# Decomposed queries and keys laid out by dimension in DRAM, narrower key loads, and the maxima stored by SyncE

## The reference

```python
q = x @ Wq
latent_kv = (x @ Wk + x @ Wv) @ W_down_kv
k_rec, v_rec = latent_kv @ W_up_k, latent_kv @ W_up_v     # 16 heads of 8 dimensions
scores = clip(einsum('bhqd,bhkd->bhqk', qh, kh) * scale)
scores = clip(scores * exp(-0.01 * 0.01 * abs(i - j)))     # decay by distance
out = softmax(scores) @ vh
```

## Time and profile before

| | us |
|---|---|
| median of 3 timed runs | 937.31 (935.65 to 938.31) |
| profiled execution, its own time | 933.09 |
| profiled execution, span of the core | 931.6 |
| TensorE busy in the span | 765.9 (82%) |
| DVE, ACT, POOL busy | 603.1, 481.9, 268.0 |
| first attention within the span | from 0 to about 450 |

### The profile page before, as it was taken

One profiled execution on the slowest core, in us unless ns is written; L12 is line 12 of the kernel. 1 busy time (PEld: TensorE's weight loads), 2 busy tenths in 40 slices (PEclk: granted clock), 3 DMA queues, 4 the chain that ended last, 5 costly groups with the idle time before them and its releaser, 6 DMA issues. The chain is left out here.

```text
span 931.6 us, 26320 instructions
## 1 busy us (share of the span) xinstructions
PE 765.9 (82%) x10923; PEld 472.2 (51%) x10923; DVE 603.1 (65%) x1402; ACT 481.9 (52%) x966; POOL 268.0 (29%) x590
## 2 busy tenths in 40 slices
PE   5469999999999999998747939999995894127990
PEld 3226555555555555554525925666653463025770
DVE  3666888888888888885362233777767445762444
ACT  4717888888878888877522543434332322001222
POOL 2547434333333343334106613000000000005531
PEclk9657999999999999998867969999999796557995
DMA  5433321111111111000292119000000003001104
GB/s 155 151 114 122 120 72 55 55 55 55 56 55 55 54 55 54 6 4 4 68 293 76 43 56 303 1 1 1 1 2 1 0 1 128 11 0 42 42 23 147
DMA packets 39319, 59.12 MB, mean 63 GB/s; under 512 B 10100, under 2 KB 21053, under 8 KB 39200
## 3 DMA queue, kind: packets, MB, share of 16 engines
q1 hardware_dynamic: 34352, 51.07, 17.0%
q0 software_dynamic: 2304, 4.74, 2.0%
q10 hardware_dynamic: 2544, 1.62, 0.6%
HBM read 42.09 MB, written 15.07 MB: 61 GB/s over the span
## 5 line engine op out<-in xcount | busy, mean ns | idle before, releaser
L857 DVE CUSTOM_DVE_ANT_0 junk<-row,rest 128x1024 bf16<-128x1024 f32 x256 | 312.7, 1225 | 71.2 <-PE row L388 53.6
L641 ACT ACTIVATE prob<-score 128x512 f32<-128x512 f32 x512 | 274.4, 598 | 89.9 <-PE score L388 89.4
L388 PE MATMUL score<-stack 75*32 75x128 bf16 (+3 forms) x3840 | 180.6, 300 | 6.1 <-DMA stack<-neg_rows 4.8
L502 PE MATMUL out_ps<-prob,v_aug 128*32 128x256 f32 x2048 | 158.4, 387 | 1.6 <-POOL prob L768 1.6
L388 PE MATMUL row<-stack 72*32 72x512 bf16 x1928 | 150.2, 387 | 0.7
L768 POOL TENSOR_SCALAR_AFFINE_SELECT prob<-prob 128x128 f32<-128x128 f32 x256 | 79.0, 309 | 199.8 <-ACT prob L641 195.2
L388 PEld LDWEIGHTS score<-stack 75*32 75x32 bf16 x3840 | 93.5, 98 | 70.2 <-ACT prob L641 15.3
L502 PEld LDWEIGHTS out_ps<-prob,v_aug 128*32 128x32 f32 x2048 | 63.4, 112 | 52.9 <-issue 2.4
L1773 POOL MEMSET ones<- 128x128 bf16 x2 | 0.4, 205 | 233.9 <-POOLq L1214 214.6
L388 PEld LDWEIGHTS row<-stack 72*32 72x32 bf16 x1928 | 48.6, 98 | 29.5 <-DVE top L857 5.2
L2006 PE MATMUL outs<-vm_w,mixed 128*64 128x256 f32 x512 | 61.7, 381 | 1.8 <-issue 1.8
(11 more groups left out here) (305 smaller groups left out, 1053.6 us busy)
## 6 DMA issues: line engine op xcount, KB each, us to landing
stack<-parts_dram SPq DMA_DIRECT2D x64, 288.0 KB
parts_dram<-prob SPq DMA_DIRECT2D x12, 256.0 KB, 7.4
parts_dram<-spare SPq DMA_DIRECT2D x12, 256.0 KB
results<-x_tok SPq DMA_DIRECT2D x12, 256.0 KB, 3.7
up_w<-in_L_ffn_w_dram SPq DMA_DIRECT2D x1, 2048.0 KB, 9.6
rows<-x_tok SPq DMA_DIRECT2D x8, 256.0 KB, 3.5
y<-results SPq DMA_DIRECT2D x8, 256.0 KB, 4.1
up_w<-in_L_ffn_wg_dram SPq DMA_DIRECT2D x1, 2048.0 KB, 10.4
```

Of the source, the lines that this page charges most:

```text
L388: last = pe.matmul(out[c:c + 32, :], keys[:, c:c + 32], queries, start=True, stop=True)
L502: last = pe.matmul(out_ps[32 * c:32 * c + 32, h // 2 * (S // 4):(h // 2 + 1) * (S // 4)], v_aug[g % 3][:, t, h, :], moving[:, :, c, :], st ...
L641: act.activation(prob[:, t, w * HALF:(w + 1) * HALF], score[n % NS][:, :], ACT.Exp).then_inc(exped, 1)
L857: dve.tensor_tensor_reduce(junk[:, slot % 2, :], row[slot % 2][:, :], rest[:, S - P - t * P:2 * S - P - t * P], 1.0, LOWEST, ALU.mult, ALU ...
```

## The change

`parts_dram` changes from (side, half, group, 24 rows, head in group, position) to (side, half, 24 rows, group, head in group, position). The projection weights are reordered so that a batch's 128 partitions go by dimension and then head, not by group, dimension and head in group. A store of one piece then writes 8 rows of 16 heads. Rows of one piece lie 64 KB apart (8 KB before). The query load keeps its form; the key load becomes three loads of 24 rows without a broadcast, and a stack's semaphore counts four DMAs (LOADS = 1 + NPART) instead of two. The table `rest` is loaded by ACT behind the ramps, at the front. `store_neg` moves from ACT to SP: heads 0, 1 and 2 between the early loads, the others between the four sides of a pair's loads in the loop. The second side of a pair (n = 1) waits for 3 units where it waited for 6. The general path addresses the new layout.

```diff
 def load_side(sp, dram, stack, pair, half, side, loaded):
-    h, group = 2 * (pair % 2), pair // 2
-    rows = dram["parts"][side, half, group, :, h:h + 2, :]
+    h, group, of = 2 * (pair % 2), pair // 2, NPART * HD
+    rows = dram["parts"][side, half, :, group, h:h + 2, :]
     if side == 0:
-        rows = rows.unsqueeze(1).to_broadcast([NPART * HD, NPART, 2, S])
+        sp.dma_start(stack[0:KR, half, 0, h:h + 2, :], rows.unsqueeze(1).to_broadcast([of, NPART, 2, S])).then_inc(loaded, 16)
     else:
-        rows = rows.unsqueeze(0).to_broadcast([NPART, NPART * HD, 2, S])
-    sp.dma_start(stack[0:KR, half, side, h:h + 2, :], rows).then_inc(loaded, 16)
-LOADS = 2
+        for a in range(NPART):
+            sp.dma_start(stack[a * of:(a + 1) * of, half, 1, h:h + 2, :], rows).then_inc(loaded, 16)
+LOADS = 1 + NPART
...
         def send_part(sp, b, half, side, k, done):
-            rows = dram["parts"][side, half, b * (NG // B):(b + 1) * (NG // B), :, :, :]
+            rows = dram["parts"][side, half, :, b * (NG // B):(b + 1) * (NG // B), :, :]
             if side == 0:
-                rows = rows[:, k * HD:(k + 1) * HD, :, :].rearrange("g r h t -> g (r h) t")
+                rows = rows[k * HD:(k + 1) * HD, :, :, :].rearrange("r g h t -> r (g h) t")
             else:
-                rows = rows.rearrange("g (r k) h t -> (g r) k h t", k=NPART)[:, k, :, :]
+                rows = rows.rearrange("(r k) g h t -> r k (g h) t", k=NPART)[:, k, :, :]
             sp.dma_start(rows, parts[b][half][:, side, k, :]).then_inc(done, 16)
...
             store_parts(sp, 0, 0, 0, 0, kept[0][0])
-            sp.dma_start(rest[:, :], io["c_rest"]).then_inc(rest_in, 16)
             for k in range(1, NPART):
...
+            def store_neg(m):
+                tile, h = of_head(m)
+                sp.wait_ge(row_done, slot_at["neg", m] + 1)
+                for half in range(2):
+                    sp.dma_start(tile[KR:KR + NPART, half, 0, h, :].rearrange("k (t c) -> k t c", c=P),
+                                 neg_rows[:, m % 2, :]).then_inc(neg_in[m % 2], 16)
...
+            store_neg(0)
             sp.wait_ge(rows_set, 2)
             for n in range(4):
                 fill_side(2, n, 0)
+            store_neg(1)
             for n in range(4):
                 fill_side(3, n, 0)
+            store_neg(2)
...
-                if pair + 3 < PAIRS:
-                    for n in range(4):
-                        fill_side(pair + 3, n, 2 * UNITS * pair + 6 * n)
+                for n in range(4):
+                    if n in (2, 3):
+                        m = 2 * pair + n - 1
+                        if n == 3 and pair + 3 < PAIRS:
+                            fill_side(pair + 3, 2, 2 * UNITS * pair + 12)
+                        if m < NH:
+                            store_neg(m)
+                    if n != 2 and pair + 3 < PAIRS:
+                        fill_side(pair + 3, n, 2 * UNITS * pair + 3 * n + (9 if n == 3 else 0))
...
             for n in range(2):
                 act.dma_start(ramp[n], io["c_ramp"][:, n, :]).then_inc(ramp_in, 16)
+            act.dma_start(rest[:, :], io["c_rest"]).then_inc(rest_in, 16)
...
-            store_neg(0)
             for step in range(LAST):
                 m, t = step // SB, step % SB
-                if t == 4 and m + 1 < NH:
-                    store_neg(m + 1)
...
             def by_head(w):
-                return w.rearrange("d (g h r) -> d g r h", h=GH, r=HD)
+                return w.rearrange("d (n r) -> d r n", r=HD)
             def by_dimension(w):
-                return w.rearrange("d (g r h) -> d g r h", h=GH, r=HD)
+                return w.rearrange("d (r n) -> d r n", r=HD)
```

More of the change, by code:

```diff
@@ L990, in _ @@
                         sp.dma_start(queries[a * NPART * HD:(a + 1) * NPART * HD, :],
-                                     parts[0, 0, g, a * HD:(a + 1) * HD, h, :].unsqueeze(0).to_broadcast([NPART, HD, S])).then_inc(loaded, 16)
+                                     parts[0, 0, a * HD:(a + 1) * HD, g, h, :].unsqueeze(0).to_broadcast([NPART, HD, S])).then_inc(loaded, 16)
                         for k in range(NPART):
                             at = (a * NPART + k) * HD
-                            sp.dma_start(keys[at:at + HD, :], parts[1, 0, g, k:NPART * HD:NPART, h, :]).then_inc(loaded, 16)
+                            sp.dma_start(keys[at:at + HD, :], parts[1, 0, k:NPART * HD:NPART, g, h, :]).then_inc(loaded, 16)
         @block.tensor
@@ L2241, in two_layers @@
             mem[f"returned{i}"] = sem(f"returned{i}")
-        dram = {"parts": nc.dram_tensor("parts_dram", (2, 2, NG, NPART * HD, GH, S), BF16, kind="Internal").ap()}
+        dram = {"parts": nc.dram_tensor("parts_dram", (2, 2, NPART * HD, NG, GH, S), BF16, kind="Internal").ap()}
         for i in range(2):
```

## The result

| | before | after |
|---|---|---|
| median of 19 timed runs of each, us | 941.27 (935.65 to 947.34) | 932.74 |
| ratio, 95% interval | | 0.9903 (0.9882 to 0.9923) |
| span of the profiled execution, us | 931.6 | 931.2 |

The change makes the kernel 9.1 us faster (7.2 to 11.1, one minus the ratio, times 941.27); forecast were 10.0.

A forecast was written before the change was run, and what follows sets the result against it. The prediction took the loop to run at TensorE's pace behind a late first score; 9.0 us from the start plus 1.0 from the loop took 937.31 to 927.3 us, range 921 to 933.

The forecast's parts named there:

- One sign of being wrong: Main loop and start: the prediction called itself wrong if TensorE stands before a head waiting for its maxima.
- Step 1: Stores of pieces to DRAM: outer dimension 8 gives 1.37 us each, bounds 0.97 and 2.7 us.
- Step 2: Key loads: one of 288 KB becomes three of 96 KB, 0.36 us each; an issue 0.79 us, perhaps 0.43.
- Step 3: Decay table at the front on ACT's queue: cost 0, at most 3.6 us lost.
- Step 4: The start, summed: key issues from 28.8, first row matmul at 32.9, first score 54.0 instead of 63.01, gain 9.0 us.
- Step 5: Main loop: stores of maxima by SP free ACT and gain 1.0 us, bounds 0 and 2.6.
- Step 7: TensorE's clock: its lag of 16.7 us behind the first score moves with the start, no further gain or loss.
- Rival A: TensorE's clock doesn't follow the start and comes back at 79.7 as before: 4.5 us lost, 931.8 us; chance 0.11.
- Rival B: Start and loop gain more: issues at 0.43 us, clock 4 us sooner, loop at its bound: 922.7 us; chance 0.10.
- C: Key loads don't spread: each 96 KB load stays at 76 GB/s, 1.3 us; 930.3 us; chance 0.05.
- D: Rows 64 KB apart in DRAM are served worse, start's stores keep 2.7 us each: 941.9 us; chance 0.05.
- E: Gain eaten behind the attention, where the clock can dip otherwise: 935 to 938 us, no change; chance 0.05.

The follow-up runs named there:

- e2: Kernel before with only each 288 KB key load split into three of 96 KB, old layout: -6.5 us (-9.6 to -3.4).
- e1: Kernel before with only the decay table loaded by ACT behind the ramps: -2.1 us (-4.8 to +0.6).
- g3: f2 with the decay table again loaded by SP behind the first store: 920.25 us, -11.7 (-14.8 to -8.4) against the kernel before.
- f1: Changed kernel with all stores of maxima issued by ACT again: -11.0 us (-14.0 to -8.1) against the kernel before.
- f2: Changed kernel with SP storing head 0's maxima between the half 1 loads of pairs 0 and 1: 918.30 us, ratio 0.9868.
- f0: Changed kernel unedited, run once more: 924.74 us against 930.13 for the kernel before, ratio 0.9933 (0.9896 to 0.997).
- before again: Kernel before unedited, run once more for a second trace: -1.1 us (-3.5 to +1.2).
- e4: Kernel before with only the stores of maxima moved from ACT to SP: +17.7 us (+13.5 to +21.8).
- e3: Kernel before with only the new DRAM layout, keys still in one broadcast load: -4.4 us (-7.1 to -1.6).
- f3: Changed kernel with room for nine groups in DRAM, rows 72 KB apart instead of 64 KB: 924.40 us, -7.2 (-10.5 to -3.7) against before.
- g2: f2 in the DRAM layout of the kernel before: 924.89 us, ratio 0.9912 (0.9881 to 0.9944) against the kernel before.

## Why the prediction was right, step by step

The forecast was 10.0 us faster, measured 9.1 and 6.2. The direction and the place (the start, and how many engines carry a transfer) were right. That the size comes so close is in part luck: the gain of the start was forecast too large, that of the loop didn't come, and a clock that came back sooner than forecast made up for some of it. The forecast time of 927.3 us was worked out from 937.31, the median of three runs; nineteen runs gave 941.27, and so 932.74 lies only just inside the range of 921 to 933. One sign of being wrong that the prediction named did come: TensorE stands 4.6 us before head 0 for its maxima, where the sum had 1 us.

Step 1, stores of 1.37 us: 1.30 measured (262,144 B at 202 GB/s). Step 2, narrow loads: issues of 0.35 us, under the lower bound (0.43) I gave; their transfers slower than 270 GB/s (168 at a share of 0.76 in e2). Step 3, table at no cost at the front: right, and worth little, as e1 and g3 show.

Step 4, the key issue at 28.8: wrong by 2.4 us. I took five stores to follow each other at 1.37 us. They nearly do so in half 1, where the queue is full (1.3 us each from 38 to 44), but not in half 0: the last lands 5.6 to 6.5 us after its issue in all versions of the new layout, where my sum had 3.5. The old layout with the table away has 5.2 to 5.7, so for half 0 the new layout brought nothing. A reason at hand is that it widens the query stores (share 0.25 alone before, 0.53 now) and narrows the key stores (in their stretch of the kernel before, 26.0 to 27.5, the share is 0.90 at 279 GB/s); no run tests this by itself. The bounds I set (0.97 to 2.7 us per store) covered the delay, but I used them as if the cost was in the engine's time per store. Three issues at 0.35 us made good for it: pair 1's issues end at 34.6, forecast 34.4. The six stores of half 1 then cost 1.5 us more than forecast: SP goes on at 46.43 and not at 44.7, since their packets pass between 36.7 and 46.0, which is 9.3 us and not 8.2, and begin 0.7 us later than I had them, beside the last loads.

Step 4, the maxima: the largest miss, 3.0 us. I had the second store land 1.7 us after its issue and the first score 2.2 us after it; the score came 5.2 us after it (53.02 to 58.23), behind eight loads in one queue. The 256-byte packets of the maxima pass between 55.42 and 56.48, so 1.75 us of the 5.2 lie behind their last byte. Without the wait (f1 and f2) the first score comes 3.9 and 3.2 us sooner than f0's on the table's scale, and the times are 5.3 and 6.4 us lower. More than the 3 to 4 us can't be put down to this wait: the attention ends only 1.5 and 0.6 us sooner than in f0's trace, 3.5 and 2.6 sooner than in the mean of the two. My text named these loads as new work in front of the maxima, counted their issues (6.4 us, measured 5.7) and forgot their bytes. Together 9.0 us were forecast and 4.8 measured in the first pair of traces; from the last key store on, over both traces of each kernel, it is 6.4.

Step 5, the loop's 1.0 us: it was next to nothing. Four heads take 47.44 to 47.47 us with and without ACT's issues (means over six groups in before, after, f0, f1, from the seventh turn of the maxima on), so that eight groups differ by some 0.2 us. The 0.13 us in one score group were not a cost repeated in each group of heads, and an ACT that is nearly full (94% with its issues) is not the bound.

Step 7, the clock: I let its lag of 16.7 us move with the first score. In the other thirteen traces it came back 8.6 to 16.7 us after the first score, but 34 to 41 us after it fell, save for before again (44.4) and e4 (51.2). The first trace of before had 47.8. So after the change the clock was back 7.4 us sooner and not 4.8, which explains most of the 6.7 us by which the attention ends sooner: (4.8 + 7.4) / 2 = 6.1, as half a us counts for each at the lower level. The clock also falls once near the end of the loop, for 6.8 us before and 3.4 us after the change, and in the second trace of either kernel not at all. Rival A, the clock back at 79.7, fell.

Rival B's cheap issues came, its other gains didn't. C fell: the loads spread (share 0.76 in e2, 0.67 here beside the maxima). D fell: stores take 1.3 us. Its argument from the single key load holds only roughly (76/3 is 25.3 GB/s per engine, 270/12 is 22.5), and rows further apart are not wholly free for the loads, as the last section shows. E came about in the one pair of profiles, by chance and not because of the shift: the wait of 3.7 us shown above is missing in the second trace of the same kernel.

What stays open: why the last five stores of half 0 need 11 to 12 us from the second one's issue to the key load (after the change the engines move 66 GB/s at a share of 0.47 from 20.7 to 22.0 and reach 199 GB/s only at 26, at about the same share); why the clock came back so soon in e3; and where the difference between 9.1 and 6.2 comes from, whose intervals overlap.

## What to carry to other kernels

Count a transfer's engines (its share of 16 in a stretch where it runs alone) before its bytes; three or four of 16 in front of a dependent small store is a chain worth breaking. A small transfer that others wait for is held by the bytes queued ahead of it and not only by their issues: give it another queue or put it ahead, both of which helped here. An engine that is freed gains nothing until it is what ends the wait. One profile each can't weigh a change of 1% when the rest of the program varies by as much; a mark behind the changed part, counted from one in front of it, can do better.

## What was unexpected

Both the narrow loads and the new layout keep the DMA engines busy for longer with the same bytes. Queue 1 on the page (packets, MB, share of 16 engines over the span) of before again:

```profile
q1 hardware_dynamic: 34352, 51.07, 17.1%
```

of e2 (narrow key loads in the old layout):

```profile
q1 hardware_dynamic: 35408, 51.08, 18.5%
```

and of f3 (new layout, padded rows), which is also what the unpadded one has:

```profile
q1 hardware_dynamic: 36944, 50.49, 18.4%
```

The 4 KB packets of the loads tell the two causes apart. Between 200 and 360 us they took 187, 193, 197 and 192 ns in the mean with wide key loads and rows 8 KB apart (before, before again, e1, e4), 206 and 209 with narrow ones (e2, g2), 216 with wide ones and rows 64 KB apart (e3), and 219 to 224 with narrow ones in the new layout, padded or not. So narrow loads cost some 3 to 22 ns a packet and rows 64 or 72 KB apart some 10 to 29, and f3's rival Q, that only the number of rows in flight matters, doesn't fit e3, whose loads are as before. Around the first score, 44 to 62 us, a packet took 222 ns before and 282 after. That more loads in flight make each packet slower fits this but was not tested by itself. In e2 from 33.5 to 35.5 only loads of 24 source rows run:

```profile
33.50:35.50 2.00, 0.00 (x0) 0.00 (x0) 0.00 (x0) 1.97 (x5) 1.94 (x2) 0.50 0.76 168
```

The Trainium skill's rule on engines per DMA (DMA: Bandwidth & Descriptors, "Why a DMA increments its semaphore by 16 and not by 1") gives how many engines take part, 12 for these loads and 8 for the new stores. The shares of 0.76 here and 0.53 for the stores agree with it. How fast each engine then is comes from the trace alone: 168 GB/s here against 270 for the single query load of the earlier trace rows, at 0.76 and 0.71.
